# A graph network on one core: the gathers of three layers wait for counts three higher

## The chip, the cores and the metric

The kernel runs on one core of a Trainium2 chip. The metric is the device time of one execution in microseconds (us). TensorE (PE) multiplies and sums in PSUM, VectorE (DVE) and ScalarE (ACT) do the elementwise work, GpSimd (POOL) issues the indirect DMAs that gather rows of a table by a list of indices, and SyncE (SP) issues the other DMAs. The engines run their own instruction streams and wait for each other through counting semaphores.

## The reference

Four graph layers over 3125 nodes of 64 features and 50,000 edges, sorted by their target node. Each layer normalises the nodes, computes something per edge from the source's row, sums it into the target, and adds the result to x.

```python
h = relu(layernorm(x))
x = x + segment_sum(h[src] @ L0_weight[type16], dst)                    # first layer
h = relu(layernorm(x))
x = x + elu((segment_sum(h[src], dst) / count) @ W_l.T + b_l + h @ W_r.T)   # mean layer
h = relu(layernorm(x))
m = silu(concat(h[src], h[dst], edge_attr) @ w1 + b1) @ w2 + b2         # messages
agg = segment_sum(m, dst)
x = x + layernorm(h + silu(concat(h, agg) @ w3 + b3) @ w4 + b4) * gamma + beta
h = relu(layernorm(x))
scores = q[dst] . key(h[src], type8), plus four rule scores             # attention
x = x + relu(layernorm(segment_sum(h[src] @ W_r[type8] * mean(softmax over dst), dst) + bias) * ln_g + ln_b)
```

## The kernel before, in words

The edges stand in 391 tiles of 128 (TE). Edges of one tile can belong to several blocks of 128 nodes, so the work goes by *slots*, one for each pair of edge tile and node block: 416 slots, in G = 52 groups of 8 (SG). One group of slots is a *step*. In a step TensorE multiplies, for each of the 8 slots, a one-hot matrix of the targets (tile `oh`, made by VectorE) with 128 edge rows, and adds the result to the sums of the slot's node block in PSUM.

The edge rows come from a table in HBM that the layer has written beforehand (for the first layer and attention it holds each node's row multiplied by each relation's matrix). GpSimd gathers them, one indirect DMA of 128 rows for each tile, in TG = 49 groups of up to 8 tiles. They land in a ring of 64 tile places, TRING = 8 groups (`got0`; `got3` in attention). The gathers carry a semaphore for each of the 8 places of the ring, `tile_gat`, and the steps wait for it. A tile group k is read by steps k to k+3 (the slots run ahead of the tiles by at most 24, three groups), so group g can overwrite group g-8 once step g-5 is done. That is the gate ahead of a group's gathers, from group 8 on. Groups 0 to 7 have none.

The semaphores of the gate count steps: `used` counts TensorE's finished steps (step s brings it to s+3 in the first layer), `edge_sum` VectorE's additions in the message layer (step s: s+2), `scored` VectorE's scores in attention (step s: s+3; VectorE's line 1037) and `values` ScalarE's copies (step s: s+1). Before the change each gate asks for what step g-5 brings.

What a step needs, by layer:
- First layer: the one-hot `oh` (line 785, which waits until the step two before is done, as there are two buffers), the landed tiles, and TensorE's 8 matmuls (16 records, line 1388). In the first 12 groups two tiles of eight are not gathered by relation: they are computed by TensorE, ScalarE and VectorE instead, so these groups have six gathers. After groups 12, 22, 32 and 42 GpSimd also issues one gather of edge attributes (line 594), up to 2 MB.
- Mean layer: gathers of its own with a gate that the change leaves alone.
- Messages: TensorE prepares the part from the target and the edge attributes (line 1511), VectorE adds the gathered rows (line 960), ScalarE applies silu, TensorE sums (line 1353). SyncE loads two small tiles for each step.
- Attention: four chunks of 16, 16, 12 and 8 steps. TensorE computes the queries (line 1576), VectorE the scores (lines 1032 to 1037), ScalarE copies the gathered values out of the ring (line 1260), and after each chunk comes its softmax. The weighted sums of a chunk's values (line 1585) run in the next chunk's steps. In the first 16 groups there are six gathers, as in the first layer.

Of the kernel before, what the change touches and what calls it, by code (L numbers as in the profile page):

```python
# [20 lines left out]
def network(nc, a, out, N, E):  # L21
# [26 lines left out]
    with ctx:  # L48
# [3 lines left out]
        def sem(name):  # L52
            return ctx.enter_context(nc.semaphore(name))
# [24 lines left out]
        values = flat[:, 0:2 * P * W].rearrange("p (s d) -> p s d", d=W)  # L78
# [104 lines left out]
        TRING = PLACES // SG  # L183
# [131 lines left out]
        def s(name):  # L315
            if name not in S:
                S[name] = sem(name)
            return S[name]
# [12 lines left out]
        def loaded(engine, row_, largest):  # L331

            _, values_ = nc.values_load_multi_w_load_instructions(  # L333
                row_, engines=[engine], min_val=0, max_val=largest,
                skip_runtime_bounds_check_because="counted on the chip from the destinations")
            return values_
# [36 lines left out]
            eng.wait_ge(tile_gat[b], 16 * (of_layers + sum(fetched(l, q) for q in range(b, k + 1, TRING))))  # L373

        EARLY = 6
        TAKE_EA = (12, 22, 32, 42)

        def groups(eng, step):
# [162 lines left out]
        def _(pool):  # L541
# [38 lines left out]
            def gather_tiles(l, k, table, dest, idx):  # L580
                for t in range(k * SG, k * SG + fetched(l, k)):
                    at_ = bass.IndirectOffsetOnAxis(ap=idx[:, t:t + 1], axis=0)
                    nc.gpsimd.indirect_dma_start(dest(t % PLACES), None, table, at_).then_inc(tile_gat[k % TRING], 16)  # L583

            for g in range(TG):
                if g >= TRING:
                    pool.wait_ge(s("used"), g - TRING + 3 + 3)
                gather_tiles(0, g, table0_d.rearrange("n (r d) -> (n r) d", d=D), lambda p: got0[:, p, 0:D], tile_idx0)
                if g in TAKE_EA:
                    c = TAKE_EA.index(g)  # L590
                    pool.wait_ge(s("ea_scratch"), 32)
                    if c:
                        pool.wait_ge(s("ea_slot_out"), 16 * c)
                    nc.gpsimd.indirect_dma_start(ea_rows[0:ROWS_OF[c], :], None, ea_d.rearrange("(t e) d -> t (e d)", e=P),
                                                 bass.IndirectOffsetOnAxis(ap=slot_ti[0:ROWS_OF[c], c:c + 1], axis=0)).then_inc(s("ea_taken"), 16)
# [8 lines left out]
            pool.wait_ge(s("plain_table_out"), 96)  # L604
            for g in range(TG):
                if g >= TRING:
                    pool.wait_ge(s("edge_sum"), g - TRING + 3 + 2)
                gather_tiles(2, g, table2_d[:, :], lambda p: got0[:, p, 0:D], tile_idx1)
            pool.wait_ge(s("plain_table_out"), 128)
            gather_ahead(3, ahead3)  # L610
# [2 lines left out]
            for k in range(TG):  # L613
                if k == 3:
                    pool.wait_ge(s("node_mm"), 20)
                    pool.wait_ge(s("qn"), 4)
                    pool.wait_ge(s("key_parts"), 1)
                if k >= TRING:
                    pool.wait_ge(s("scored"), k - TRING + 3 + 3)
                    pool.wait_ge(s("values"), k - TRING + 3 + 1)  # L620
                gather_tiles(3, k, table3_d.rearrange("n (r d) -> (n r) d", d=2 * D), lambda p: got3[:, p, :], tile_idx3)


# [1 line left out]
        def _(dve):  # L625
# [21 lines left out]
            def table_half(n):  # L647
                dve.wait_ge(s("tab_ps"), 2 * n + 1)
                stage_free(dve, 0, n)
                V.tensor_copy(stage[:, n % 4, 0:512], acc[:, (n % 2) * 1024:(n % 2) * 1024 + 512]).then_inc(s("tabA"), 1)  # L650
# [56 lines left out]

            for n in range(EARLY):
                table_half(n)
# [421 lines left out]
        def _(act):  # L1131
# [27 lines left out]
            for n in range(NT):  # L1159
                stage_free(0, n)  # L1160
                at_ = (n % 2) * 1024
                if n == EARLY:
                    act.wait_ge(s("tabA"), EARLY)
                if n >= EARLY:
                    act.wait_ge(s("tab_ps"), 2 * n + 1)
# [125 lines left out]
        def _(pe):  # L1291
# [41 lines left out]
            def table_ps(l, n):  # L1333
                hf = slice((n % 2) * D, (n % 2) * D + D)
                lhs = hT[hf, n // 2, :]
                if l == 0:
                    at_ = (n % 2) * 1024
                    for r, freed in enumerate(("tabA", "tabB")):
                        if n >= 2:
                            pe.wait_ge(s(freed), n - 1)  # L1340
                        T.matmul(acc[:, at_ + 512 * r:at_ + 512 * r + 512], lhs, w0[hf].rearrange("p r d -> p (r d)")[:, 512 * r:512 * r + 512], start=True, stop=True).then_inc(s("tab_ps"), 1)  # L1341
                else:
                    if n >= 4:
                        pe.wait_ge(s("tabB"), NT + n - 3)
                    T.matmul(acc[:, (n % 4) * 512:(n % 4) * 512 + 512], lhs, wr3[hf].rearrange("p r d -> p (r d)"), start=True, stop=True).then_inc(s("tab_ps"), 1)
# [52 lines left out]
            pe.wait_ge(s("w0_in"), 32)  # L1398
            for n in range(EARLY):
                table_ps(0, n)  # L1400
# [4 lines left out]
            last.then_inc(s("rows_ps"), 1)  # L1405
            for n in range(EARLY, LATE):
                table_ps(0, n)
# [258 lines left out]
```

## Time and profile before

| | us |
|---|---|
| runs | 2657.2 and 2665.6 |
| median | 2661.4 |
| span of the profiled execution, first to last instruction | 2690.8 |
| GpSimd busy in it | 1543.2 (57%) |
| TensorE busy in it (matmuls) | 1523.2 (57%) |
| VectorE busy in it | 1051.5 (39%) |
| ScalarE busy in it | 487.3 (18%) |

For the profiled execution only the span is known; it is 1.1% above the median of the two runs. All numbers of the rows below are from it. In the profile an indirect gather counts as busy on GpSimd while its descriptors are made; the rows land later.

### The profile page before, as it was taken

Reading aid. Unit: us, or ns where it says so; the run is one execution under the profiler, and the core shown is the slowest. Engines: PE = TensorE matmul, PEld = TensorE weight load, DVE = VectorE, ACT = ScalarE, POOL = GpSimd, SP = SyncE. Lnnn points to the kernel's source line nnn. Section 1 sums busy time; section 2 is a strip of 40 time slices with the busy share of each in tenths; the row PEclk is TensorE's granted clock in tenths of the full one; section 3 lists DMA queues with packets and bytes.
Section 4 is the critical chain, followed back from the end, with each engine's and each line's share of the span. In section 5 each row is a group of like instructions: output and inputs, shape, how many; then the busy total and the mean of one; then the engine's idle time right before and its main releaser. Section 6 shows DMA issues by size and latency. Waiting matters only on the chain.

```text
span 2690.8 us, 27765 instructions
## 1 busy us (share of the span) xinstructions
PE 1523.2 (57%) x8443; PEld 1343.0 (50%) x8443; DVE 1051.5 (39%) x2213; ACT 487.3 (18%) x1153; POOL 1543.2 (57%) x1509
## 2 busy tenths in 40 slices
PE   5545332424478888765376667659553536445564
PEld 2224332424367777765376666658332325435554
DVE  4446110111556565633122222223524634334467
ACT  2100000000356666501000000001211111001020
POOL 5447766764667777735566666662344556665620
PEclk8656555555677777766555655657656766666677
DMA  6432122120111111103122222222341212222210
GB/s 199 130 110 86 24 84 58 36 61 16 30 31 36 34 37 34 33 12 65 37 52 50 57 51 51 58 51 44 110 162 52 65 54 66 61 55 68 58 39 13
DMA packets 159861, 159.26 MB, mean 59 GB/s; under 512 B 108361, under 2 KB 111993, under 8 KB 158748
## 3 DMA queue, kind: packets, MB, share of 16 engines
q1 hardware_dynamic: 111372, 89.07, 11.7%
q0 software_dynamic: 48352, 68.42, 11.5%
q8 instruction: 79, 1.29, 0.2%
q14 instruction: 58, 0.48, 0.1%
HBM read 118.71 MB, written 46.06 MB: 61 GB/s over the span
## 4 chain that ended last, share of the span: by engine, by line
another core or an unknown queue 30%; DVE 21%; PE 17%; issue 16%; POOL 10%; DVEq 2%; ACT 1%; DMA 1%; SPq 1%; ACTq 0%; POOLq 0%
POOL flat L583 10%; DVE flat L824 7%; PE ps L1353 4%; DVE oh L785 2%; DVE oh L1043 2%; PE ps L1388 2%; PE ps L1511 2%; DVE msg L1034 2%; DVEq L333 1%; PE ps L1341 1%; DVE msg L960 1%; DVE ohT L791 1%; PE ps L1325 1%; PE ps L1509 1%
## 5 line engine op out<-in xcount | busy, mean ns | idle before, releaser
L583 POOL DMA_INDIRECT flat<-table,flat x1061 | 1122.8, 1058 | 639.7 <-issue 314.7
L1388 PE MATMUL ps<-flat,oh 128*128 x1664 | 328.9, 380 | 368.1 <-DVE oh L785 255.3
L785 DVE TENSOR_TENSOR oh<-iota_n,drel 128x1024 f32<-128x1024 f32 x156 | 190.1, 1223 | 867.8 <-remote 605.0
L1388 PEld LDWEIGHTS ps<-flat,oh 128*128 128x128 f32 x1664 | 314.3, 291 | 394.7 <-issue 392.7
L583 POOL DMA_INDIRECT flat<-table,tile_idx x359 | 346.7, 966 | 267.9 <-DVE base L1037 140.2
L1353 PE MATMUL ps<-msg,oh 128*128 128x64 f32 x832 | 173.3, 393 | 156.5 <-ACT msg L1209 135.4
L1353 PEld LDWEIGHTS ps<-msg,oh 128*128 128x128 f32 x832 | 166.6, 304 | 160.4 <-issue 160.4
L1366 PE MATMUL ps<-uvT,flat 128*128 128x192 bf16 x2200 | 229.3, 275 | 25.7 <-ACT flat L1191 17.2
L1366 PEld LDWEIGHTS ps<-uvT,flat 128*128 128x128 bf16 x2200 | 219.8, 112 | 34.6 <-issue 29.3
L1576 PE MATMUL ps<-qn,ohT 128*128 x832 | 159.0, 349 | 124.9 <-issue 104.0
L1511 PEld LDWEIGHTS ps<-uvT,ohT 128*128 128x128 f32 x832 | 178.3, 291 | 64.3 <-issue 48.9
L1576 PEld LDWEIGHTS ps<-qn,ohT 128*128 128x128 f32 x832 | 143.4, 258 | 132.7 <-issue 132.1
L824 DVE TENSOR_TENSOR flat<-flat,iota_node 128x1536 bf16<-128x1536 f32 x110 | 193.2, 1757 | 3.0
L1511 PE MATMUL ps<-uvT,ohT 128*128 x832 | 166.1, 361 | 48.2 <-issue 48.2
L1187 ACT ACTIVATE flat<-flat,iota_node 128x512 bf16<-128x512 f32 x220 | 146.8, 714 | 170.8 <-DMA flat<-tile_source 105.5
L1585 PE MATMUL ps<-flat,oh 128*128 128x65 f32 x704 | 115.0, 329 | 70.7 <-DVE oh L1043 45.5
L1585 PEld LDWEIGHTS ps<-flat,oh 128*128 128x128 f32 x704 | 112.6, 248 | 76.2 <-issue 76.2
L1191 ACT ACTIVATE flat<-flat 128x512 bf16<-128x512 bf16 x220 | 126.4, 621 | 3.5
L1260 ACT COPY flat<-flat 128x64 f32 x416 | 65.8, 241 | 271.7 <-DMA flat<-table,tile_idx 209.3
L1032 DVE COPY rule_e<-ps 128x32 f32<-128x32 f32 x52 | 9.8, 188 | 269.2 <-remote 225.1
L1203 ACT COPY flat<-ps 128x256 f32<-128x256 f32 x52 | 19.3, 373 | 528.4 <-remote 360.4
L1509 PE MATMUL ps<-flat 128*128 128x256 f32 x208 | 105.0, 602 | 9.7 <-issue 9.4
(320 smaller groups left out, 1481.9 us busy)
## 6 DMA issues: line engine op xcount, KB each, us to landing
table<-flat SPq DMA_DIRECT2D x52, 512.0 KB
drow<-slot_node SPq DMA_DIRECT2D x104, 256.0 KB
flat<-table,flat POOLq DMA_INDIRECT x1061
flat<-edge_attr_by_slot SPq DMA_DIRECT2D x52, 128.0 KB
edge_attr_padded<-edge_attr SPq DMA_DIRECT2D x1, 6250.0 KB
flat<-table,tile_idx POOLq DMA_INDIRECT x359
flat<-tile_source SPq DMA_DIRECT2D x22, 256.0 KB
edge_attr_by_slot<-flat SPq DMA_DIRECT2D x2, 2048.0 KB
```

The lines of the kernel that those rows point to most:

```text
L583: nc.gpsimd.indirect_dma_start(dest(t % PLACES), None, table, at_).then_inc(tile_gat[k % TRING], 16)
L785: V.tensor_tensor(oh[:, b], iota_n[:].unsqueeze(1).broadcast_to([P, SG, P]), drel[:, g * SG:(g + 1) * SG].unsqueeze(2).broadcast_to([P, SG ...
L824: V.tensor_tensor(src_oh[:, m % BINS, 0:ON_DVE, :], src_row[:, b].unsqueeze(1).broadcast_to([P, ON_DVE, PICK * P]), iota_node[:, CH * c:CH ...
L1187: last = A.activation(src_far[:, k - ON_DVE], src_row[:, q % 2], ACT.Square, bias=iota_node[:, t:t + 1], scale=-1.0)
L1191: last = A.activation(src_oh[:, m % BINS, k, :], src_far[:, k - ON_DVE], ACT.Relu, bias=1.0, scale=-1.0)
L1353: last = T.matmul(acc[:, bass.ds(n[j] * D, D)], oh[:, b, j, :], rows_[:, j, :], start=False, stop=True, skip_group_check=True)
L1366: last = T.matmul(picked_ps[b][:, j], src_oh[:, m % BINS, k, j * P:(j + 1) * P], h_parts[:, :, t, :], start=(t == 0 and j % 2 == 0), stop= ...
L1388: last = T.matmul(acc[:, bass.ds(n[j] * pitch + shift, width)], oh[:, b % 2, j, :], got[:, bass.ds(place[j], width)], start=False, stop=Tr ...
L1509: T.matmul(eb[b % 2][:, 256 * q:256 * q + 256], eaT[:, b % 2, q, :], w1c.rearrange("p s d -> p (s d)"), start=True, stop=False, skip_group ...
L1511: last = T.matmul(eb[b % 2][:, j * D:(j + 1) * D], ohT[:, b % 2, j, :], v[:, bass.ds(n[j], 1), :].rearrange("p t d -> p (t d)"), start=Fal ...
L1576: last = T.matmul(qr_ps[g % 2][:, j // 4, j % 4], ohT[:, b % 2, j, :], qn_room[:, bass.ds(n[j] * QR, P)], start=True, stop=True)
L1585: last = T.matmul(acc[:, bass.ds(n[j] * PITCH + SHIFT, W)], oh[:, b % 2, j, :], values[:, bass.ds(lw * SG + j, 1), :].rearrange("p s d -> ...
```

## The change

Each of the gates ahead of a group's gathers in the first layer, the message layer and attention asks for a count three higher, which is that of step g-2. No instruction is added or removed, and all stand in the same order on every engine; the line numbers after the new constant rise by one. The mean layer's gate, the ring and its places stay as they are. VectorE and ScalarE, where they write into the ring themselves (first 12 and 16 groups), keep waiting for step g-5.

```diff
         EARLY = 6
+        AHEAD = 3
         TAKE_EA = (12, 22, 32, 42)
...
             for g in range(TG):
                 if g >= TRING:
-                    pool.wait_ge(s("used"), g - TRING + 3 + 3)
+                    pool.wait_ge(s("used"), g - TRING + 3 + 3 + AHEAD)
                 gather_tiles(0, g, table0_d.rearrange("n (r d) -> (n r) d", d=D), lambda p: got0[:, p, 0:D], tile_idx0)
...
                 if g >= TRING:
-                    pool.wait_ge(s("edge_sum"), g - TRING + 3 + 2)
+                    pool.wait_ge(s("edge_sum"), g - TRING + 3 + 2 + AHEAD)
                 gather_tiles(2, g, table2_d[:, :], lambda p: got0[:, p, 0:D], tile_idx1)
...
                 if k >= TRING:
-                    pool.wait_ge(s("scored"), k - TRING + 3 + 3)
-                    pool.wait_ge(s("values"), k - TRING + 3 + 1)
+                    pool.wait_ge(s("scored"), k - TRING + 3 + 3 + AHEAD)
+                    pool.wait_ge(s("values"), k - TRING + 3 + 1 + AHEAD)
                 gather_tiles(3, k, table3_d.rearrange("n (r d) -> (n r) d", d=2 * D), lambda p: got3[:, p, :], tile_idx3)
```

## Rows read from the trace of the kernel before

**Rows 1.** The page's costliest group: line engine op, out<-in xcount | busy, mean ns | idle before.

```profile
L583 POOL DMA_INDIRECT flat<-table,flat x1061 | 1122.8, 1058 | 639.7 <-issue 314.7
```

**Rows 2.** GpSimd's waits: us, times, longest. The last line is window 220 to 646.

```profile
POOL flat L583 <- DVE base L1037: 140.2, 20, 25.3
POOL flat L583 <- DVE msg L960: 95.7, 18, 18.1
...
POOL flat L583 <- remote: 29.5, 6, 7.6
```

**Rows 3.** Line 583 by stretch: us, POOL busy (x), PEclk, DMA share, GB/s.

```profile
220.00:644.00 424.00, 297.42 (x296) 0.51 0.23 57
1332.00:1838.00 506.00, 331.97 (x327) 0.55 0.27 54
2070.00:2575.00 505.00, 300.97 (x311) 0.64 0.23 61
```

**Rows 4.** Timeline, first layer: start, us, what, [idle before]. Group 8's first gather; step 6.

```profile
186.12 0.95 POOL L583 DMA_INDIRECT flat<-table,flat  x1 [27.97 <-PE ps L1388]
...
205.09 2.00 PE L1388 MATMUL ps<-flat,oh 128*128 x16 [1.63 <-issue]
```

**Rows 5.** Timeline, first layer: last gather of group 28; steps 27 and 28.

```profile
416.56 0.95 POOL L583 DMA_INDIRECT flat<-table,flat  x1 [0.30 <-issue]
...
409.25 3.67 PE L1388 MATMUL ps<-flat,oh 128*128 x16 [6.33 <-DMA flat<-table,flat]
419.27 3.67 PE L1388 MATMUL ps<-flat,oh 128*128 x16 [6.35 <-DMA flat<-table,flat]
```

**Rows 6.** Timeline, first layer: one-hots of steps 29 to 32; groups 33 and 34 begin.

```profile
424.29 1.23 DVE L785 TENSOR_TENSOR oh<-iota_n,drel 128x1024 f32<-128x1024 f32 x1 [20.10 <-PE ps L1388]
464.19 1.23 DVE L785 TENSOR_TENSOR oh<-iota_n,drel 128x1024 f32<-128x1024 f32 x1 [38.68 <-remote]
478.39 2.36 DVE L785 TENSOR_TENSOR oh<-iota_n,drel 128x1024 f32<-128x1024 f32 x2 [12.97 <-remote]
...
464.43 1.82 POOL L583 DMA_INDIRECT flat<-table,flat  x1 [5.59 <-remote]
...
478.62 1.81 POOL L583 DMA_INDIRECT flat<-table,flat  x1 [3.62 <-remote]
```

**Rows 7.** Timeline, end of the first layer: last gather of group 48; steps 47 to 51.

```profile
643.25 0.95 POOL L583 DMA_INDIRECT flat<-table,flat  x1 [0.30 <-issue]
...
652.54 17.32 PE L1388 MATMUL ps<-flat,oh 128*128 x80 [21.61 <-DVE oh L785]
```

**Rows 8.** Timeline, messages: group 8's first gather; VectorE's additions of step 4.

```profile
1331.90 1.21 POOL L583 DMA_INDIRECT flat<-table,flat  x1 [18.06 <-DVE msg L960]
...
1339.35 1.14 DVE L960 TENSOR_TENSOR msg<-ps,flat 128x64 f32<-128x64 f32 x8
```

**Rows 9.** Timeline, messages, one cycle: first gathers of two bursts, VectorE between.

```profile
1704.50 1.21 POOL L583 DMA_INDIRECT flat<-table,flat  x1 [3.54 <-DVE msg L960]
...
1709.99 1.14 DVE L960 TENSOR_TENSOR msg<-ps,flat 128x64 f32<-128x64 f32 x8
...
1727.51 1.23 DVE L785 TENSOR_TENSOR oh<-iota_n,drel 128x1024 f32<-128x1024 f32 x1 [15.72 <-remote]
...
1730.06 1.21 POOL L583 DMA_INDIRECT flat<-table,flat  x1 [4.94 <-DVE msg L960]
```

**Rows 10.** Timeline, TensorE in the message layer's first burst; one row of many alike.

```profile
1283.87 0.26 PE L1511 MATMUL ps<-uvT,ohT 128*128 x1 [2.54 <-issue]
```

**Rows 11.** Timeline, attention: group 8's first gather, and that of a later burst.

```profile
2069.70 0.95 POOL L583 DMA_INDIRECT flat<-table,tile_idx  x1 [25.28 <-DVE base L1037]
...
2272.79 1.21 POOL L583 DMA_INDIRECT flat<-table,tile_idx  x1 [5.03 <-DVE base L1037]
```

**Rows 12.** Timeline, attention's last chunk: scores of steps 44 and 45.

```profile
2596.27 0.69 DVE L1037 TENSOR_REDUCE base<-msg 128x8 f32<-128x512 f32 x1
2602.90 0.69 DVE L1037 TENSOR_REDUCE base<-msg 128x8 f32<-128x512 f32 x1
```

## Prediction

> **What bounds the kernel now.** I read the page first: the costliest group by far is GpSimd's (POOL's) indirect gather of line 583, 1061 of them for the first three layers, 1122.8 us [rows 1]. A gather takes 0.95 us and the next begins 0.30 us later [rows 5], so a group of eight costs 10.0 us. The view of who waits for whom then says what stops GpSimd at the gates that the change touches: DVE L1037 in attention (140.2 us), DVE L960 in messages (95.7 us), and in the first layer "remote", a release whose cause the profile does not find (29.5 us) [rows 2].
>
> Next I cut the span into the three stretches in which the gates act: groups 12 to 48 of the first layer in 424 us, groups 8 to 48 of messages in 506 us and of attention in 505 us [rows 3]. Per group this is 424/37 = 11.5, 506/41 = 12.3 and 505/41 = 12.3 us, against 10.0 us of bare issue. The step rate follows GpSimd there. With GpSimd silent, steps are faster: five first-layer steps in 17.32 us (3.5 each) [rows 7], a message step in some 8.9 us (step 3 releases GpSimd just before 1331.90, step 4 ends at 1340.5) [rows 8], an attention step in 6.6 us [rows 12].
>
> The timeline shows why GpSimd stops at all. **First layer:** TensorE waits for landings and runs one step in 10 us [rows 5]. VectorE's one-hot for step s+2 needs only the end of step s. After step 27 (ends 412.9) it starts at 424.29, after step 28 (422.9) at 464.19, and after step 29 (one step time later, 433) at 478.39 [rows 5, 6]. So TensorE's signals arrive 11, 41 and 45 us late while GpSimd issues without a pause. GpSimd runs on through its lead, stops at 458.8 (group 33 needs step 28), starts again at 464.43 the moment the signal arrives, and one group later stops for another 3.62 us [rows 6]. **Messages:** a burst of two groups, 1704.50 to 1725.1, then 4.94 us of pause; VectorE, which had waited 15.72 us for TensorE, goes on 2.4 us after the burst ends [rows 9]. In the layer's first long burst TensorE itself issues one matmul in 2.8 us (2.54 of them idle) [rows 10]. **Attention** shows the same pause, 5.03 us [rows 11]. I take as the working rule that a long unbroken run of gathers holds TensorE up, and that its signals come through 2 to 6 us after the run ends.
>
> **The change.** No instruction is added, removed or moved; four constants rise by three. The gather of group g now waits for the end of step g-2, not g-5. Groups 0 to 7 have no gate, and the mean layer keeps its own.
>
> (a) *First layer, restart.* Group 8 starts at 186.12, when step 3 ends; step 6 ends at 205.09 + 2.00 = 207.1 [rows 4]. GpSimd sets the pace behind it, so 21 us are lost, less some 2 us because groups 8 to 11 (six gathers, 7.5 us each) run near step pace anyway: 19 us.
>
> (b) *First layer, tail.* After GpSimd's last gather (ends 644.2) TensorE's last five steps end at 669.9, 25.7 us later [rows 7]. After the change group 48 is issued when step 46 is done, and steps 47 to 51 remain, with a landing or a late signal before them: 17.3 + 2 to 6 us, about 22. Gain 4 us.
>
> (c) *First layer, pace.* A group is used 1.8 us after its last gather was issued (417.5 to 419.27) [rows 5]: two groups of lead (20 us) cover a landing. What is not covered is the lateness. Now GpSimd pays for it 5.6 + 3.6 us [rows 6] about once in nine groups, because five groups of lead bridge 40 us. With two it stops within a group. From below: it stops just as seldom, 11.5 us per group, +0. From above: the pace of the message layer, two groups and a pause, 12.3 us: 37 x 0.8 = +30 us. Worse is one group per pause, as between 464.43 and 478.62 [rows 6], 14.2 us: 37 x 2.7 = +100 us. I take +20, nearer the message layer than nothing, since both other layers are in that cycle, and since the first late signal, which now costs GpSimd nothing, will stop it. The edge-attribute gathers (L594), four in this layer, delay the landings behind them; today lead hides that, and what shows of it is inside the 20.
>
> (d) *Messages.* Group 8 starts at 1331.90, after step 3; at 8.9 us a step [rows 8] step 6 ends near 1358, so GpSimd starts 26 us later, but three more steps are done. From there steps and groups go one for one, at 12.3 us. At the end three fewer steps remain when the gathers are over: 3 x 8.9 us less. 26 - 26 = 0. The cycle of two survives the shorter lead: the second step of a pair ends 1711.1 - 1704.5 = 6.6 us after the restart, inside the 10 us of the group then being issued [rows 9], so the next group is free in time; and the pause ends as now, by the late step, 5 us after the burst.
>
> (e) *Attention.* Group 8 starts at 2069.70 after step 3 [rows 11]. At 6.6 us a step [rows 12] step 6 ends near 2089: 19 us later for GpSimd, three steps won, as in (d). At the end the last chunk, today without gathers, gets groups 46 to 48: three steps at landing pace (10 us of issue and 2 of landing) for 6.6 us, and a pause of 5: 3 x 5.4 + 5 = 21 us. Three steps at the start now run at 6.6 us instead of 12.3: 17 us. Sum +4.
>
> Sum: 19 - 4 + 20 + 0 + 4 = +39 us. The profiled span is 2690.8 us and the median of the runs 2661.4, 1.1% less; a difference of this size carries over unscaled, so the forecast is **2700 us** (+1.5%), a span near 2730.
>
> A rule of the Trainium skill speaks against the change. Its page "DMA: Bandwidth & Descriptors", section "Rules for kernel authors", says to issue a DMA early and to wait for it late. By [rows 5] that matters only where less than a landing is left; two groups leave 20 us, so the rule alone would add nothing to (a). The page "SBUF — State Buffer", section "SBUF: two separate sides", says that among the engines only VectorE and GpSimd can block each other, for the length of one instruction, and that TensorE and ScalarE never wait. The gather beside a one-hot, 1.82 us against 0.95 [rows 5, 6], agrees; the 40 us of lateness and the 2.8 us matmuls [rows 6, 10] lie outside that rule, and the measurement decides.
>
> **Rivals.**
> *Faster: short bursts keep TensorE awake.* If TensorE is held up only by long unbroken runs, a GpSimd that stops earlier might never hold it up. The waits of the locked parts would go: 95.7 - 18.1 = 78 us in messages, 140.2 - 25.3 = 115 us in attention (half of it, 58, since part of it stands in the softmax between chunks), and 29.5 us in the first layer [rows 2]. With the 19 us of (a), 2661 - 146 = 2515 us in full, about 2600 for somewhat less than half. For it: the signals in the first few us of a burst come at once (step at 1709.99) [rows 9]. Against: the second group is free after 6.6 us in either kernel, so bursts stay at two groups.
> *Slower: one group per pause in the first layer.* A late signal stops GpSimd after one group, the pause lets one step through, and the restart catches TensorE again, as at 464.43 [rows 6]: +100 in (c) instead of +20, 2780 us. It decides if a pause of 4 us does not clear what TensorE has pending; the second pause, at 478.62, did. A milder form, the first layer at 12.3 us per group and both other layers at 12.8, gives 2661 + 49 + 82 x 0.5 = 2750.
> *The gates do nothing:* something else would be stopping GpSimd. The 18 and 20 waits on DVE L960 and L1037 [rows 2] speak against it; only if fewer stalls win (a) back does the time stay at 2661.
>
> **How the numbers follow.** Forecast, 2675 to 2725: 0.45. Nothing or a small gain, 2630 to 2675: 0.20. Faster rival, 2515 to 2608: 0.13. Slower rivals, 2725 to 2790: 0.22. A measurement of this kernel tells 2% (53 us) from no change: faster 0.13; slower than 2714.6: 0.22 and a quarter of the forecast's share, 0.33; within: 0.54. The range reaches from the small gain to the milder slow case: 2630 to 2760.
>
> **What would show it.** Right: GpSimd's restarts near 207, 1358 and 2089; in the first layer more pauses of 3 to 6 us and no lateness of 40 us; a pause of 5 us after each two groups in messages and attention; gathers in attention's last chunk. Wrong: message steps under 12 us each while gathers run (the faster rival), or first-layer groups 14 us apart (the slower one).

## The result, and the profile after

The changed kernel takes 2704.0 us (median of 2 runs, 2703.0 and 2705.0) against 2661.4 us: ratio 1.0158, 95% interval 1.009 to 1.0226. The ratios here and below leave out executions in which the chip ran in a slower state, so they need not equal the quotient of the medians. Its profiled execution has a span of 2701.2 us. That of the kernel before was 2690.8 us, long for its runs, so the two spans differ by 10 us only where the medians differ by 43; lengths of layers are therefore compared over several profiles below.

The line numbers are one higher. The page's costliest group of the kernel after, which answers to [rows 1]:

```profile
L584 POOL DMA_INDIRECT flat<-table,flat x1061 | 1130.0, 1065 | 662.6 <-issue 311.4
```

GpSimd's waits after (us, times, longest), beside [rows 2]:

```profile
POOL flat L584 <- DVE base L1038: 164.9, 22, 40.2
...
POOL flat L584 <- DVE msg L961: 106.2, 16, 38.4
...
POOL flat L584 <- PE ps L1389: 74.9, 8, 49.5
...
POOL flat L584 <- remote: 57.9, 27, 4.0
```

The last two over the whole span of the kernel before, since [rows 2] has "remote" for a window only:

```profile
POOL flat L583 <- remote: 52.0, 19, 7.6
POOL flat L583 <- PE ps L1388: 50.7, 9, 28.0
```

The longest member of each of the first three has grown, from 25.3, 18.1 and 28.0 us to 40.2, 38.4 and 49.5. They are the gates of group 8, in the timeline after (start, us, what, [idle before]):

```profile
207.25 0.94 POOL L584 DMA_INDIRECT flat<-table,flat  x1 [49.45 <-PE ps L1389]
...
1369.17 1.21 POOL L584 DMA_INDIRECT flat<-table,flat  x1 [38.38 <-DVE msg L961]
...
2110.75 0.94 POOL L584 DMA_INDIRECT flat<-table,tile_idx  x1 [40.19 <-DVE base L1038]
```

In the first layer that is the end of step 6, on TensorE of the same profile:

```profile
204.98 2.00 PE L1389 MATMUL ps<-flat,oh 128*128 x16
```

From there to the last gathers, by stretch (us, POOL busy (x), PEclk, DMA share, GB/s), beside [rows 3]:

```profile
207.00:673.00 466.00, 327.39 (x319) 0.51 0.22 53
1369.00:1868.00 499.00, 335.68 (x327) 0.55 0.27 54
2110.00:2626.00 516.00, 302.42 (x311) 0.65 0.24 61
```

Groups 8 to 48 are 41 groups: 11.4, 12.2 and 12.6 us per group. Counted in the same way from group 8, the kernel before has 11.2, 12.3 and 12.3, so no layer's pace has changed by more than 0.3 us per group. In the first layer VectorE's one-hots now look like this in the timeline:

```profile
402.01 1.23 DVE L786 TENSOR_TENSOR oh<-iota_n,drel 128x1024 f32<-128x1024 f32 x1 [11.66 <-remote]
417.59 1.23 DVE L786 TENSOR_TENSOR oh<-iota_n,drel 128x1024 f32<-128x1024 f32 x1 [14.35 <-remote]
419.47 1.22 DVE L786 TENSOR_TENSOR oh<-iota_n,drel 128x1024 f32<-128x1024 f32 x1 [0.65 <-PE ps L1389]
437.16 1.23 DVE L786 TENSOR_TENSOR oh<-iota_n,drel 128x1024 f32<-128x1024 f32 x1 [16.47 <-remote]
452.78 1.23 DVE L786 TENSOR_TENSOR oh<-iota_n,drel 128x1024 f32<-128x1024 f32 x1 [14.39 <-remote]
454.77 1.22 DVE L786 TENSOR_TENSOR oh<-iota_n,drel 128x1024 f32<-128x1024 f32 x1 [0.76 <-PE ps L1389]
```

and GpSimd's pauses in the same stretch:

```profile
417.82 1.81 POOL L584 DMA_INDIRECT flat<-table,flat  x1 [3.79 <-remote]
...
453.01 1.80 POOL L584 DMA_INDIRECT flat<-table,flat  x1 [3.83 <-remote]
```

The idle time of 38.68 us that [rows 6] show is gone; behind group 8 the longest in the layer is 18.3 us. GpSimd here stops after three groups for 3.8 us, and in the 2 us around its restart VectorE gets the signals of two steps (417.59 and 419.47, 452.78 and 454.77). The end of the layer, last gather and the last steps:

```profile
669.85 0.94 POOL L584 DMA_INDIRECT flat<-table,flat  x1 [0.30 <-issue]
...
672.77 13.91 PE L1389 MATMUL ps<-flat,oh 128*128 x64 [10.30 <-DMA flat<-table,flat]
```

The last four steps stand together behind the last landing, 15.9 us in all; before it was 25.7 us [rows 7]. And attention's last chunk, which had no gathers, now has three groups: two behind a long pause and the last behind a second one:

```profile
2589.36 1.21 POOL L584 DMA_INDIRECT flat<-table,tile_idx  x1 [22.71 <-DVE base L1038]
2616.79 1.21 POOL L584 DMA_INDIRECT flat<-table,tile_idx  x1 [6.94 <-DVE base L1038]
```

### The profile page after: what moved, and what is told of

Read it like the earlier page. It is cut to its first block, busy times and chain, and to the rows that moved or that the text cites. A ratio compares the mean times of both kernels' runs of the same rounds, so it can differ in the third digit from the quotient of the medians.

```text
span 2701.2 us, 27765 instructions
## 1 busy us (share of the span) xinstructions
PE 1537.9 (57%) x8443; PEld 1352.0 (50%) x8443; DVE 1053.1 (39%) x2213; ACT 487.5 (18%) x1153; POOL 1551.3 (57%) x1509
## 4 chain that ended last, share of the span: by engine, by line
another core or an unknown queue 28%; DVE 20%; PE 19%; issue 17%; POOL 12%; DVEq 2%; ACT 1%; DMA 1%; SPq 1%; ACTq 0%; POOLq 0%
POOL flat L584 12%; DVE flat L825 6%; PE ps L1354 4%; PE ps L1389 2%; DVE oh L1044 2%; PE ps L1512 2%; DVE oh L786 2%; DVE msg L1035 1%; DVEq L333 1%; PE ps L1510 1%; PE ps L1326 1%; PE ps L1367 1%; PE ps L1342 1%; DVE ohT L792 1%
## 5 line engine op out<-in xcount | busy, mean ns | idle before, releaser
L584 POOL DMA_INDIRECT flat<-table,tile_idx x359 | 347.8, 969 | 291.8 <-DVE base L1038 164.9
```

## The experiments

They ran in four sets, each set on one chip with the kernel before beside it. The first set met a chip unlike that of the result, so parts of it were run again.

**First set: one gate at a time, and all.** Each of three kernels has the three higher counts in one layer only; the fourth is the changed kernel. The first layer's edit:

```diff
-                    pool.wait_ge(s("used"), g - TRING + 3 + 3)
+                    pool.wait_ge(s("used"), g - TRING + 3 + 3 + AHEAD)
```

> The later gate in the first layer alone. By the sum of the prediction this layer carries nearly the whole loss: +19 (restart) - 4 (tail) + 20 (pace) = +35 us, 2696 us, ratio 1.013. The traces of the change and of before put it at +18 us (first gather of the layer to its last step 571.9 us before, 589.6 us after). The theory that the layer's loss is only the later restart of group 8 says +15 to +21 us, with the pace per group as before (11.5 us). The rival that late signals of TensorE cost more with less lead says over +30 us.

> The later gate in the message layer alone. The prediction says 0 us: three steps are won at the start for the three groups that GpSimd is late, and the cycle of two groups and a pause stays. The traces say +7 us (648 to 655 us from first gather to last step). Rival, the short lead breaks the cycle to one group per pause: +80 us or more.

> The later gate in attention alone. The prediction says +4 us; the traces say -16 us (653 to 637 us from first gather to last step), which would be the three steps at the start run at 6 us each while GpSimd is silent, with little of it lost in the last chunk. If the gain is by chance of how the pauses fell, the timed runs show about 0 (ratio within 0.003 of 1).

> The changed kernel once more, on the same chip as its three parts. If the parts do not interact, its difference to before is the sum of theirs. The two spans say +10 us, the medians of two runs +43 us; one of the two is an accident of the runs. From the traces (+18, +7, -16 and some 3 us elsewhere) I expect +10 to +15 us, ratio 1.005.

Measured, with the kernel before at 2230.1 us here, not 2661: first layer alone 2241.3 us, ratio 1.0049 (1.0022 to 1.0076); messages alone 2229.1, 0.9997 (0.9976 to 1.0018); attention alone 2233.2, 1.0018 (0.9992 to 1.0044); all three 2247.5, 1.0080 (1.0059 to 1.0102). The whole level is 16% lower, and the profile says where. Messages in the kernel with attention's gate alone (so this layer is the code of before), first long run of gathers: TensorE in the timeline, then line 1512 by stretch (us, PE busy, PEld busy, PEclk, DMA share, GB/s):

```profile
1115.32 1.81 PE L1512 MATMUL ps<-uvT,ohT 128*128 x8
1116.92 1.17 PE L1510 MATMUL ps<-flat 128*128 128x256 f32 x2
1117.88 1.81 PE L1512 MATMUL ps<-uvT,ohT 128*128 x8
```

```profile
1109.00:1169.00 60.00, 20.81 (x94) 22.56 (x94) 0.50 0.32 66
```

The same layer and line of the kernel before, on the chip of the result:

```profile
1256.00:1316.00 60.00, 3.76 (x16) 3.83 (x15) 0.50 0.17 32
```

In 60 us of unbroken gathers 94 of these matmuls against 16, at the same granted clock (0.50, the 1.2 GHz level). So the clock is not the difference: in this stretch TensorE isn't held up beside the gathers. The other profiles agree: from 25 to 85 us behind the layer's first gather, the seven with TensorE held up and no gate ahead of group 8's have 13 to 21 of these matmuls, the seven without the hold-up 87 to 96. The chain of work that ended last is then GpSimd's at 60% in the kernel with attention's gate alone (first line, shares by engine), while the kernel after in its first profile has GpSimd at 12% (second line):

```profile
POOL 60%; issue 20%; PE 9%; DVE 5%; DMA 5%; SPq 1%; ACT 1%; ACTq 0%; DVEq 0%; POOLq 0%
```

```profile
another core or an unknown queue 28%; DVE 20%; PE 19%; issue 17%; POOL 12%; DVEq 2%; ACT 1%; DMA 1%; SPq 1%; ACTq 0%; POOLq 0%
```

In the kernels with one gate here, GpSimd waits at the first layer's gate of group 8 for 14.7 us and hardly again, at no gate of messages, and three times (7.9 us) at attention's, none of them group 8's. So the first layer loses a late start, messages nothing, and attention at most those three waits. The forecasts for these kernels, of +35 or +18 us for the first layer, were made for a chip like that of the result and are not tested by it.

**Second set: the kernel before again, and gates for groups 2 to 7.** The second kernel adds waits where there were none: groups 2 to 7 wait for step g-2; from group 8 on all is as before. The first layer's edit, with its like in messages and attention:

```diff
-                if g >= TRING:
-                    pool.wait_ge(s("used"), g - TRING + 3 + 3)
+                if g >= 2:
+                    pool.wait_ge(s("used"), g - TRING + 3 + 3 + (0 if g >= TRING else 3))
```

> The kernel before, unchanged. On the chip of the first four runs it took 2230 us, and in those traces TensorE issued its matmuls without delay beside the gathers and GpSimd hardly ever paused; in the trace of before that the prediction read, it took 2691 us. If the delay of TensorE beside unbroken gathers belongs to the chip, this run shows either about 2230 us with no GpSimd pause over 1 us in the three gated layers, or about 2660 us with some 50 of them, and nothing between.

> Before, with gates for groups 2 to 7 too: they wait for step g-2, so that each layer's first run of 48 or 64 gathers is broken up; from group 8 on the waits are those of before. Where TensorE is held up by unbroken gathers (the trace of before), steps 1 or 2 of the three layers no longer stand still for 36 to 65 us: 30 to 100 us faster. Where it is not held up, GpSimd only loses what it waits in the first groups: 10 us in the first layer (its steps 0 and 1 come late), little in the others: ratio 1.00 to 1.01.

Measured: before 2670.6 us, again 2671.2, ratio 0.9998 (0.9965 to 1.003). The early gates take 2658.9 us, ratio 0.9945 (0.9911 to 0.9978): faster, by 12 to 15 us, and far less than the 30 to 100 us expected. The timeline of messages in that kernel, GpSimd's two first stops and VectorE's second and third step:

```profile
1269.47 1.21 POOL L583 DMA_INDIRECT flat<-table,flat  x1 [6.31 <-DVE msg L960]
1291.61 1.21 POOL L583 DMA_INDIRECT flat<-table,flat  x1 [0.50 <-DVE msg L960]
```

```profile
1268.07 1.14 DVE L960 TENSOR_TENSOR msg<-ps,flat 128x64 f32<-128x64 f32 x8
1276.61 1.14 DVE L960 TENSOR_TENSOR msg<-ps,flat 128x64 f32<-128x64 f32 x8
```

In the kernel before, the second step's one-hot waits through the first run of gathers:

```profile
1322.46 1.23 DVE L785 TENSOR_TENSOR oh<-iota_n,drel 128x1024 f32<-128x1024 f32 x1 [65.08 <-remote]
```

A pause of 6 us in that run gets steps done that otherwise stand still for 65 us. It doesn't shorten this layer, though: in the one profile messages take 648.7 us, within the 648.4 to 655.0 of the old gates. The first layer takes 561.2 us, just below the 563.1 to 571.8 without early gates, and attention 626.8, below 633.0 to 652.9; most of the gain seems to lie there. And in the first layer one-hots still wait up to 41.5 us later on, so the early gates break up only the first run.

**Third set: the parts again.** The chip of the second set was given again, so the same four kernels as in the first set could be timed with TensorE held up.

> Only the first layer's gate asks for three more; messages and attention are the code of before. The same kernel as in the first set of runs, again, in case this chip is one on which TensorE is held up beside GpSimd (before near 2660). There the traces of before and after say that the first layer loses 18 us: expected +18 (ratio 1.007), with group 8 some 21 us later and pauses of 3 to 6 us every three or four groups. Rival: the loss is all in the profiled execution's luck and the layer is as long as before (ratio 1.000). If the chip is not of that kind (before near 2230), +11 as before (1.005).

> Only the message layer's gate asks for three more. On a chip on which TensorE is held up: +7 us by the two traces (ratio 1.003), restart of group 8 some 35 us later, most of it won back by the three steps done. Rival: 0. On a chip without it: 1.000.

> Only attention's gate asks for three more. On a chip on which TensorE is held up: the two traces say -16 us (ratio 0.994). Rival: those 16 us belong to an unlucky profiled execution of before, and attention by itself gives +4 as the prediction had it (1.002) or more. On a chip without it: 1.002.

> All three gates, the changed kernel again. On a chip on which TensorE is held up: 1.016 as first measured; if the parts add up, it is the sum of the three kernels beside it. Rival: it is slower than their sum, because a layer's later end shifts what overlaps between layers. On a chip without it: 1.008.

Measured, beside 2663.7 us for before:

| | us | ratio | 95% interval |
|---|---|---|---|
| first layer alone | 2693.3 | 1.0117 | 1.0079 to 1.0155 |
| messages alone | 2672.9 | 1.0017 | 0.9976 to 1.0058 |
| attention alone | 2677.5 | 1.0047 | 0.9998 to 1.0095 |
| all three | 2692.5 | 1.0099 | 1.0064 to 1.0134 |

The first layer alone costs as much as all three, and more than the 1.007 expected. Added up, the parts give 1.8% and the three gates together 1.0%; with about 0.4 points of noise on each, that gap is at the edge of what these runs can tell, and no run explains it. (In the first set it was 0.6% against 0.8%.) The -16 us that the first two profiles gave attention, a ratio of 0.994, is refuted: it lies below the interval of attention alone.

Now there are seven profiles with TensorE held up and each layer with one gate or the other: the kernel before twice, the changed one twice, and three with one part. Each layer from its first gather to its last step, cut at group 8's first gather and at the last gather (starts and ends in the timelines, means over the profiles in us; 4 with the old gate, 3 with the new):

| | to group 8 | to the last gather | to the last step | sum |
|---|---|---|---|---|
| first layer, old gate | 88.4 | 458.2 | 19.9 | 566.6 (563.1 to 571.8) |
| first layer, new gate | 110.0 | 465.0 | 15.9 | 590.9 (589.6 to 591.6) |
| messages, old | 101.5 | 503.2 | 47.1 | 651.7 (648.4 to 655.0) |
| messages, new | 122.0 | 502.6 | 31.7 | 656.3 (647.3 to 666.6) |
| attention, old | 83.6 | 501.3 | 60.1 | 645.0 (633.0 to 652.9) |
| attention, new | 100.6 | 514.7 | 23.7 | 639.0 (637.1 to 641.8) |

The changes are +24.3, +4.6 and -6.1 us, together +23. The first layer's lies far outside the spread, the other two within it. Behind group 8's gate GpSimd stops 5 to 7 times for more than 1 us in the first layer with the old gate, 28 to 35 us in all, and 11 to 13 times with the new one, 36 to 42 us in all. In the mean that is 8 us more, about what the middle column has gained.

**Fourth set: the late start alone, and narrow rows.** In the first kernel only groups 8, 9 and 10 of the first layer wait for three more steps:

```diff
-                    pool.wait_ge(s("used"), g - TRING + 3 + 3)
+                    pool.wait_ge(s("used"), g - TRING + 3 + 3 + (AHEAD if g < TRING + 3 else 0))
```

> In the first layer only the gates of groups 8, 9 and 10 ask for three more (steps 6, 7 and 8); from group 11 on the gate is that of before (step g-5), and messages and attention are the code of before. Theory: the first layer's loss is the restart. Group 8 starts some 22 us later and GpSimd sets the pace behind it, so the layer stays some 20 us longer though the lead of five groups is back: ratio 1.007 to 1.008 on a chip on which TensorE is held up (before near 2660), and 1.004 to 1.005 on one on which it is not (before near 2230). Rival: the loss is the short lead later in the layer, and a late start is made up for by fewer and shorter pauses: 1.000 to 1.002.

Measured, on a chip without the hold-up (before 2229.5 us): 2240.6 us, ratio 1.0056 (1.0038 to 1.0074), as much as the 1.0049 that the first layer's whole change cost on such a chip. GpSimd's only stop at a gate of this layer that is longer than 1 us:

```profile
145.96 0.94 POOL L584 DMA_INDIRECT flat<-table,flat  x1 [13.44 <-PE ps L1389]
```

The layer takes 501.2 us in this profile, from the first gather at 69.7 us to the last step's end at 570.9, against 491.7 with the old gate and 507.2 with the new one throughout (means of two profiles each). By the profiles the late start is 9.5 us of 15.5, by the medians all of it; its profiled execution was the fastest of its nine. So the lead of five groups comes back and makes up for little or nothing: where GpSimd sets the pace, what its start loses is lost. That holds for this chip; with TensorE held up the kernel wasn't run.

The second kernel leaves out 56 of the 64 columns of each row that messages gather:

```diff
-                gather_tiles(2, g, table2_d[:, :], lambda p: got0[:, p, 0:D], tile_idx1)
+                gather_tiles(2, g, table2_d.rearrange("n (r d) -> (n r) d", d=8), lambda p: got0[:, p, 0:8], tile_idx1)
```

> Code of before, but in the message layer each gathered row is 8 floats wide and not 64; the other 56 columns of a ring place keep what an earlier layer left there, so the layer's messages are not those of the reference. As many gathers and as many rows, an eighth of the bytes. It asks what holds TensorE up beside GpSimd's gathers. Theory: the issue of the gathers by itself, so on a chip on which TensorE is held up the message layer stays near 650 us and TensorE issues a matmul every 2.8 us in the first burst as before. Rival: the bytes that land hold it up, and the layer falls by 50 to 120 us towards the 528 us that it takes on a chip without the hold-up. On such a chip the run says only whether landings set the pace there: 528 us if not.

Measured: 2252.5 us, ratio 1.0120 (1.0091 to 1.0148). The chip has no hold-up, so the question of what causes it stays open. What the run does tell is of GpSimd: its gathers in messages by stretch (us, POOL busy (x), PEclk, DMA share, GB/s), narrow rows first, then whole rows in the kernel with attention's gate alone:

```profile
1085.00:1603.00 518.00, 398.94 (x391) 0.54 0.26 43
```

```profile
1083.00:1584.00 501.00, 381.89 (x391) 0.53 0.33 67
```

391 gathers each; the narrow ones take 1.02 us against 0.98 and the layer's gathers 17 us more. An eighth of the bytes saves nothing, so the bytes are not the limit there. Why a gather of fewer bytes takes longer to issue wasn't found, nor why the runs differ by 23 to 27 us where the gathers explain 17.

## Why the prediction was right

2700 us was forecast and 2704.0 measured. That the two are 4 us apart is partly luck: the forecast adds 39 us, the first two runs gave +43, but the repeat with more runs gave 1.0099 (+26 us) and the layers of seven profiles +23. The direction, the leading term and the layer that carries the loss are right: the first layer lost 24 us of a forecast 35, and the other two together gained 1 us where 4 were to be lost. The steps, with TensorE held up:

(a) *Restart in the first layer*, forecast +19 (21 late, 2 made good). Group 8 starts at 207.25 us, with 207 foretold, and in the mean of the profiles 21.6 us later in its layer. Right, and of about the size of the layer's whole loss; whether some 2 us are made good the splits don't show. The late start by itself shows it as the cause of most or all of the loss on the other kind of chip.

(b) *Tail*, forecast -4, measured -4.0 in the mean, but the match is luck. The forecast went from 25.7 to about 22 us; the tail after is 15.9 us in all three profiles, and the one before varies from 15.9 to 25.7, mean 19.9. The last steps ran together right behind the last landing, without the late signal and the fifth step that the forecast allowed for.

(c) *Pace in the first layer*, forecast +20, the term that was mis-sized: 458.2 to 465.0 us, +7. It lies in the bounds of 0 to +30. The prediction put the first layer near messages' cycle of two groups and a pause. It came mostly to three or four groups and a pause of 3.2 us in the mean instead, a little over 11 us per group. There are more pauses, as foretold, but they are shorter and nearly make up for the fewer long ones of before: in each, TensorE's held signals come through, and VectorE's longest idle time ahead of a one-hot, behind group 8, falls from 36 to 40 us to 18 or 19. In the profiles of before and after the pauses behind group 8's add up to 34 us (7 pauses) and 36 (11); over all seven profiles they grew by 8 us.

(d) *Messages*, forecast 0 from +26 at the start and -26 at the end. Measured +20.6, -0.6 and -15.4: +4.6, within the spread, and 1.0017 (0.9976 to 1.0058) by itself. The cycle stayed too, though it is one of two or three groups and a pause in either kernel (14 to 19 pauses with the old gate, 14 to 16 with the new). Group 8 came at 1369, not 1358; 17 us of that are the layer's later start, which the forecast of 1358 didn't add, and counted from the start of the layer it came 6 us sooner than forecast.

(e) *Attention*, forecast +4. Measured +17.0 at the start, +13.3 between and -36.4 at the end, -6.1 in all, and by itself 1.0047 (0.9998 to 1.0095), +13 us. The signs disagree, both are within what these runs can tell, and so is +4. The last chunk got gathers and pauses, as foretold, though one pause was of 22.71 us where 5 were allowed for. Its length isn't all loss: the last gather comes 30 us later in the layer, and the last scores follow it at 24 us, not at 60.

The rivals. *Faster*: refuted as forecast. It would have removed GpSimd's waits for VectorE behind group 8's; they are 68 us and 125 us in the profile after (106.2 - 38.4 and 164.9 - 40.2), against 78 and 115, and the bursts in messages stayed at two or three groups. A grain of it is true: stopping GpSimd earlier in the *first* burst of each layer, with the lead kept later, gained 0.55%. *Slower, one group per pause*: refuted, 11.4 us per group, not 14.2. *The gates do nothing*: refuted by the waits of 49.45, 38.38 and 40.19 us at group 8.

The rule of the Trainium skill (page "DMA: Bandwidth & Descriptors", section "Rules for kernel authors": issue early, wait late) was weighed as adding nothing to (a). On the chip without the hold-up the first layer still lost 15.5 us (first gather to last step, 491.7 us with the old gate and 507.2 with the new, two profiles each), most of it or all by the late start. Issuing later cost time there, but through GpSimd's own pace and not through a landing that came too late, of which alone the prediction's reading of the rule took account.

## What to carry to other kernels

A tighter gate on a ring costs most at its first use, where the ring's free places let the gathering engine run unhindered: if that engine then sets the pace, little or nothing of the late start was made up here. Once both were in a cycle, the shorter lead cost 7 us in 458 in the first layer, with more and shorter pauses, and nothing clear of the noise in the other two. Split a layer at its first gate, its last gather and its last step, and average such splits over several profiles before putting a few us down to one part: one pair of profiles gave attention -16 us, and the mean of seven -6.

If TensorE stands still in the first run of gathers, gates for the groups that have none, with the full lead afterwards, are worth trying: 0.9945 (0.9911 to 0.9978) here, with TensorE held up.

## What the runs showed of the hardware that was not expected

- Whether TensorE is held up beside GpSimd's gathers went with the chip. One chip, used for two sets, held it up both times. In the result's runs and two sets it was (before 2661, 2671 and 2664 us), in two others it wasn't (2230 and 2230), with the same program. One line's matmuls in 60 us: 16 against 94 at the same granted clock of 0.50. The change costs 1.0 to 1.6% on the one and 0.8% on the other, so its sign doesn't hang on it, though 16% of the time does.
- The page "SBUF — State Buffer" of the Trainium skill, section "SBUF: two separate sides", has TensorE and ScalarE never wait for another engine at SBUF's ports. The chip without the hold-up agrees (in the stretch above TensorE stops only for ScalarE's results, about 1 us per step); on the other, TensorE issues a matmul per 2.8 us there [rows 10]. What holds it up, and why on some chips only, none of the runs shows.
- Gathering an eighth of the bytes per row took 1.02 us per gather and not 0.98, and the kernel 1.2% longer.
